# Sends of the negated maxima moved from ScalarE to SyncE, and the step tables of a fused attention kernel shifted

## The chip, the cores and the metric

The kernel runs on one core of a Trainium2 chip. Its engines are PE (TensorE, the matmuls; its weight loads are listed as PEld), DVE (VectorE), ACT (ScalarE), POOL (GpSimd) and SP (SyncE, here the engine that issues the transfers). Each works through its own list in order; semaphores tie the lists together. The metric is the device time of one execution in microseconds; lower is better.

## What is computed

Sixteen sequences of 128 rows and 256 columns go through two attentions and two feed-forward layers. The change touches the first attention, which works across columns: per sequence eight heads, each of 16 of the 128 rows.

```python
def _L0_xattn_ref(q, k, v):                 # q: layernorm(x); k = v = ctx_2048; 8 heads
    qh = q.reshape(b * h, d // h, m)
    kh = k.reshape(b * h, d // h, -1)
    vh = v.reshape(b * h, c // h, -1)
    qk = jnp.einsum('bdm,bdn->bmn', qh, kh) * scale
    sm = jax.nn.softmax(qk, axis=-1)
    ret = jnp.einsum('bmn,bcn->bcm', sm, vh)
x = x + _L0_xattn_ref(_layernorm(x), ctx_2048, ctx_2048)
x = x + _L0_ffn_ref(_layernorm(x), ...)     # 16 experts, top-k tokens for each
x = x + _L1_xattn_ref(_layernorm(x), ctx_2048, mask)
x = x + _L1_ffn_ref(_layernorm(x), ...)     # top-k rows, gelu
```

## The kernel before

A batch is one sequence, a unit is two batches (NU = 8 units), a step is one head of one batch: 16 steps to a unit, LAST = 128 steps in all. Stage A runs them. Each engine has its own unrolled loop over t, and in step t

- PE computes scores of step n = `ahead(t)` into `score_bank` (two matmuls; n is t + 24 from t = 16 on, two n per step for t of 8 to 15), then the transposed scores of step t + 2 into `scoret_bank` (`scores_t`, which waits for the exponential of step t), and every fourth step, after the exponential of step t, sixteen small matmuls for probabilities times values (`values`, into `pv_bank`). So scores of unit w start at PE's step 24, 40, 56, 72, 88 for w = 3 to 7, and step 12 for w = 2.
- DVE takes the row maximum of the scores of step n (`maximum`), and once per batch divides (`gather_parts`, `invert`, `bring_over`), makes statistics and scales rows.
- ACT does the exponential of step t from `scoret_bank` (`exponential`), then whatever copies are due.
- POOL does subtractions, roots and additions.

The transposed scores need the maxima as two extra rows of `q_stack`. PE transposes a batch's maxima (`max_t`) into `t0_bank`, ACT writes the high bf16 part of their negative (`neg_high`), DVE the low part (`neg_low`), and two DMAs carry both into `q_stack` (`send_neg_max`, L884 to L887). In before ACT issues these two DMAs itself, in its step MAX_T + 3, after waiting for `neg_low`. `scores_t` of a batch's first step waits for them (PE step 8b - 2).

The other input of the scores are stacks: q and k of a unit are each split into three bf16 parts. k: `high_k` on ACT, `rest_k` on POOL, `mid_k` on ACT, `low_k` on POOL. q: `scale_q` on DVE, `high_q`, `rest_q`, `mid_q`, `low_q` likewise. SP writes the parts to DRAM (`write_k_parts`, `write_q_parts`), fetches the next unit's rows (`load_stage`), waits until the parts are written and loads them back as stacks in nine DMAs (`load_stacks`). PE's first scores of a unit wait for these nine.

When each of these is due is set by hand, in tables of step numbers (L51 to L58): `MAX_T` for a batch's `max_t`, `STAGE` for `high_k`, `rest_k` and the statistics of a unit, `MID_K`, `SCALE_Q`, `HIGH_Q`, `MID_Q` for the splits, `CTX_T` and `TAKE_VT` for the transposed context. Each loop asks `due(table, t)`, with an offset of its own. In before SP has no steps: its order is unit by unit. Which engine reaches a step first is up to the semaphores; the tables fix only the order on each engine.

## Time and profile before

| | us |
|---|---|
| median of 3 runs (451.76 to 454.36) | 451.77 |
| the profiled execution, its time | 453.62 |
| its span on the core | 451.8 |
| PE busy in it | 293.6 (65%) |
| DVE busy | 298.2 (66%) |
| ACT busy | 170.7 (38%) |
| POOL busy | 113.1 (25%) |

The profile is one execution. Times are us from the start of the span unless marked ns; a row of the timeline is the start, the duration, the engine, the line of the kernel and output<-inputs, with the engine's idle time before it and what ended it in brackets. A "q" behind an engine's name is its sequencer, which issues DMAs. Stage A's exponentials run from 44.37 to about 266; a search for a threshold follows until about 326, then the second attention and the last layer. Line numbers are those of before, unless said otherwise.

### The profile page before, as it was taken

Reading aid. Unit: us, or ns where it says so; the run is one execution under the profiler, and the core shown is the slowest. Engines: PE = TensorE matmul, PEld = TensorE weight load, DVE = VectorE, ACT = ScalarE, POOL = GpSimd, SP = SyncE. Lnnn points to the kernel's source line nnn. Section 1 sums busy time; section 2 is a strip of 40 time slices with the busy share of each in tenths; the row PEclk is TensorE's granted clock in tenths of the full one; section 3 lists DMA queues with packets and bytes.
Section 4 is the critical chain, followed back from the end, with each engine's and each line's share of the span. In section 5 each row is a group of like instructions: output and inputs, shape, how many; then the busy total and the mean of one; then the engine's idle time right before and its main releaser. Section 6 shows DMA issues by size and latency. Waiting matters only on the chain.

```text
span 451.8 us, 6847 instructions
## 1 busy us (share of the span) xinstructions
PE 293.6 (65%) x1888; PEld 185.2 (41%) x1888; DVE 298.2 (66%) x925; ACT 170.7 (38%) x413; POOL 113.1 (25%) x248
## 2 busy tenths in 40 slices
PE   0053764777667878767986764100157999999996
PEld 0011422343333443434442422000135888888884
DVE  6855565457666875768775453888747788878641
ACT  3201632334554465534354651000011455565622
POOL 1101662233322434222122221000013333332300
PEclk9999966668888695899685995555555799999999
DMA  3876584662925719245000047000000000000001
GB/s 97 194 186 113 137 166 83 155 107 93 159 49 146 135 51 180 54 114 111 0 2 1 3 127 245 1 1 0 0 0 1 1 23 2 23 23 23 23 25 46
DMA packets 24106, 32.80 MB, mean 73 GB/s; under 512 B 3915, under 2 KB 22158, under 8 KB 22542
## 3 DMA queue, kind: packets, MB, share of 16 engines
q1 hardware_dynamic: 23566, 32.34, 31.4%
q10 hardware_dynamic: 512, 0.13, 0.2%
q8 instruction: 12, 0.20, 0.2%
q14 instruction: 16, 0.13, 0.1%
HBM read 23.88 MB, written 8.39 MB: 71 GB/s over the span
## 4 chain that ended last, share of the span: by engine, by line
DVE 33%; PE 33%; issue 11%; DMA 8%; ACT 5%; ACTq 4%; POOL 4%; SPq 2%; DVEq 1%; POOLq 0%
PE pv_bank L1054 7%; DVE row_max L574 6%; DVE denom_inv L592 5%; PE scoret_bank L1040 4%; ACTq L886 4%; DMA q_stack<-q_parts_dram 4%; PE t_bank L1237 4%; PE score_bank L1027 4%; PE pv_bank L1155 3%; ACT probs L875 2%; DMA q_parts_dram<-q_parts 2%; PE score_bank L1218 2%; POOL rstd L390 2%; DVE junk L685 1%; DVE denom_own L596 1%
## 5 line engine op out<-in xcount | busy, mean ns | idle before, releaser
L574 DVE TENSOR_REDUCE row_max<-score_bank 128x2 f32<-128x512 f32 x112 | 73.5, 675 | 65.0 <-PE score_bank L1027 64.6
L875 ACT ACTIVATE probs<-scoret_bank 128x512 f32<-128x512 f32 x128 | 74.2, 600 | 77.0 <-issue 50.8
L1040 PE MATMUL scoret_bank<-q_stack,k_stack 98*128 98x256 bf16 x256 | 61.1, 332 | 53.4 <-ACT probs L875 44.5
L1027 PE MATMUL score_bank<-k_stack,q_stack 96*128 96x256 bf16 x240 | 57.7, 337 | 23.3 <-DMA q_stack<-q_parts_dram 16.1
L1040 PEld LDWEIGHTS scoret_bank<-q_stack,k_stack 98*128 98x128 bf16 x256 | 24.8, 114 | 75.7 <-ACT probs L875 57.6
L1054 PE MATMUL pv_bank<-probs,values_ones 128*32 128x256 f32 x512 | 48.6, 514 | 0.0
L1027 PEld LDWEIGHTS score_bank<-k_stack,q_stack 96*128 96x128 bf16 x240 | 21.4, 114 | 56.5 <-DVE row_max L574 21.5
L388 POOL TENSOR_SCALAR var_eps<-mv 128x1 f32<-128x1 f32 x48 | 9.1, 190 | 137.1 <-DVE mv L743 78.3
L1155 PE MATMUL pv_bank<-q_stack,k_stack 128*128 (+1 forms) x256 | 35.8, 283 | 0.4 <-ACT q_stack L1003 0.4
L978 ACT COPY xnt<-score_bank 128x256 f32<-128x256 f32 x16 | 6.0, 373 | 75.4 <-PE score_bank L1176 75.4
L1155 PEld LDWEIGHTS pv_bank<-q_stack,k_stack 128*128 128x128 f32 x256 | 33.7, 201 | 1.3 <-issue 0.9
L404 POOL TENSOR_TENSOR x_new<-gathered,xs 128x256 f32<-128x256 f32 x16 | 11.6, 722 | 73.4 <-DVE gathered L599 68.4
L1237 PE MATMUL t_bank<-k_stack,probs 128*128 128x256 f32 x128 | 29.4, 382 | 0.0
L390 POOL TENSOR_TENSOR rstd<-var_eps,minus_half 128x1 f32<-128x1 f32 x48 | 26.3, 549 | 9.1 <-POOL var_eps L388 9.1
L592 DVE RECIPROCAL denom_inv<-gathered 128x256 f32<-128x256 f32 x16 | 27.9, 1744 | 0.1
L1237 PEld LDWEIGHTS t_bank<-k_stack,probs 128*128 128x128 f32 x128 | 23.7, 190 | 2.9
L1054 PEld LDWEIGHTS pv_bank<-probs,values_ones 128*32 128x32 f32 x512 | 16.3, 133 | 19.2 <-issue 15.0
L1136 PE MATMUL t_bank<-count,same_expert 128*128 128x3 bf16 x15 | 2.8, 186 | 31.8 <-DVE equal L685 31.8
L997 ACT ACTIVATE probs<-pv_bank,b1s 128x128 f32<-128x128 f32 x64 | 17.6, 379 | 11.8 <-PE pv_bank L1155 11.7
L1083 PE MATMUL t_bank<-wr_moving,xnt 128*128 128x272 f32 x64 | 18.6, 415 | 1.2 <-ACT xnt L927 1.2
L1070 PE MATMUL t_bank<-ident,ctx_stage 128*128 128x128 f32 x32 | 7.2, 367 | 16.2 <-DMA x_stage<-in_x_dram 16.2
L586 DVE SCALAR_TENSOR_TENSOR gathered<-pv_bank,high,low_part 128x512 f32<-128x512 f32 x16 | 11.9, 742 | 6.3 <-ACT low_part L921 6.3
(191 smaller groups left out, 542.2 us busy)
## 6 DMA issues: line engine op xcount, KB each, us to landing
q_stack<-q_parts_dram SPq DMA_DIRECT2D x48, 128.0 KB, 7.0
k_parts_dram<-k_parts SPq DMA_DIRECT2D x24, 128.0 KB
q_parts_dram<-q_parts SPq DMA_DIRECT2D x24, 128.0 KB
k_stack<-k_parts_dram SPq DMA_DIRECT2D x8, 384.0 KB, 4.9
ctx_stage<-in_ctx_dram SPq DMA_DIRECT2D x8, 256.0 KB, 3.3
x_stage<-in_x_dram SPq DMA_DIRECT2D x8, 256.0 KB, 4.2
k_stack<-k_parts_dram SPq DMA_DIRECT2D x8, 256.0 KB, 5.5
xs<-in_x_dram SPq DMA_DIRECT2D x8, 256.0 KB, 7.8
```

The lines of the kernel that those rows point to most:

```text
L390: pool.tensor_tensor(dst, work, minus_half[:, 0:dst.shape[1]], ALU.pow).then_inc(s[ready], 1)
L574: dve.tensor_reduce(row_max[:, i, :, h], score_bank[bank_of][:, :].rearrange("p (m n) -> p m n", m=2), AX.X, ALU.max).then_inc(s["max_done ...
L592: dve.reciprocal(denom_inv[:, i, :], gathered[:, i, 0, :]).then_inc(s["div_step"], 1)
L875: act.activation(probs[:, j % PROBS, :], scoret_bank[j % 2][:, :], ACT.Exp).then_inc(s["exp_done"], 1)
L886: act.dma_start(q_stack[QROWS + part:QROWS + part + 1, u % SLOTS, :, i, :], neg_max[:, i, part, :]).then_inc(neg_loaded[i], 16)
L997: act.activation(hid[:, h, :], hid_bank[h // 4][:, (h % 4) * P:(h % 4 + 1) * P], ACT.Gelu_apprx_tanh, bias=b1s[:, h:h + 1]).then_inc(s["f_ ...
L1027: ins = pe.matmul(to[:, m * D:(m + 1) * D], q_stack[0:QROWS, slot, h, b_in, m * P:(m + 1) * P], k_stack[0:QROWS, slot, h, b_in, :], start= ...
L1040: ins = pe.matmul(scoret_bank[j % 2][:, k * D:(k + 1) * D], k_stack[0:SROWS, slot, h, b_in, k * P:(k + 1) * P], q_stack[0:SROWS, slot, h, ...
L1054: ins = pe.matmul(pv_bank[i][pair * Q:(pair + 1) * Q, odd * D:(odd + 1) * D], values_ones[:, i, k, pair, odd, :], probs[:, (j - GROUP + 1 ...
L1083: pe.matmul(t1_bank[:, 0:D + NE], xnt[:, i, k, :], wr_moving[:, k, :], start=(k == 0), stop=False)
L1155: ins = pe.matmul(hid_bank[h // 4][:, (h % 4) * P:(h % 4 + 1) * P], w1s[:, k, h * P:(h + 1) * P], zg[:, k, bass.ds(P * t, P)], start=(k == ...
L1237: ins = pe.matmul(y_bank[:, 0:D], hid[:, h, :], w2s[:, h, :], start=(h == 0), stop=(h == NF - 1))
```

## The change

`send_neg_max` becomes a function of SP. SP's loop over units becomes a loop over the steps: it sends a batch's maxima two steps behind `neg_low`, writes k parts in step MID_K, writes q parts and loads the next unit's rows in step MID_Q, and loads the stacks two steps later. The tables get new numbers; the high and the low part of the maxima get tables of their own (`NEG_HIGH` for ACT, `NEG_LOW` for DVE).

```diff
-MAX_T = {1: 1, 2: 9, 3: 15, **{b: NH * b - 13 for b in range(4, NB)}}
-STAGE = {3: 9, 4: 21, **{w: STEPS * (w - 3) for w in range(5, NU)}}
-MID_K = {2: 0, 3: 11, 4: 23, **{w: STAGE[w] + 3 for w in range(5, NU)}}
-SCALE_Q = {2: 1, 3: 11, 4: 24, **{w: STAGE[w] + 6 for w in range(5, NU)}}
-HIGH_Q = {2: 3, 3: 13, 4: 25, **{w: STAGE[w] + 7 for w in range(5, NU)}}
-MID_Q = {2: 5, 3: 15, 4: 27, **{w: STAGE[w] + 9 for w in range(5, NU)}}
-CTX_T = {2: 5, 3: 12, 4: 23, **{w: STAGE[w] + 7 for w in range(5, NU)}}
-TAKE_VT = {2: 7, 3: 13, 4: 25, **{w: STAGE[w] + 9 for w in range(5, NU)}}
+MAX_T = {1: 0, 2: 9, 3: 16, 4: 21, **{b: NH * b - 14 for b in range(5, NB)}}
+NEG_HIGH = {b: MAX_T[b] + 3 for b in MAX_T} | {1: 1}
+NEG_LOW = {b: MAX_T[b] + 2 for b in MAX_T} | {1: 1, 2: 10}
+STAGE = {3: 10, 4: 22, 5: 35, 6: 50, 7: 66}
+MID_K = {2: 0, **{w: STAGE[w] + 3 for w in STAGE}}
+SCALE_Q = {2: 0, 3: 12, 4: 25, 5: 40, 6: 55, 7: 71}
+HIGH_Q = {2: 4, **{w: SCALE_Q[w] + 4 for w in STAGE}}
+MID_Q = {w: HIGH_Q[w] + 3 for w in HIGH_Q}
+CTX_T = {2: 4, 3: 13, 4: 31, 5: 39, 6: 55, 7: 71}
+TAKE_VT = {2: 6, 3: 15, 4: 34, 5: 42, 6: 58, 7: 74}
...
-            sp.wait_ge(neg_loaded[0], 32)
+            send_neg_max(0, 0)
             load_x(0)
             load_small()
...
+            for t in range(LAST):
+                for b in due(NEG_LOW, t - 2):
+                    send_neg_max(b // 2, b % 2)
+                for w in due(MID_K, t):
+                    write_k_parts(w)
+                for w in due(MID_Q, t):
+                    write_q_parts(w)
+                    if w + 1 < NU:
+                        load_stage(w + 1)
+                for w in due(MID_Q, t - 2):
+                    load_stacks(w, w >= SLOTS)
+                if t % STEPS == STEPS - 4 and t // STEPS + 1 < NU:
+                    wait_apart(sp, s["x_loaded"], 16 * (t // STEPS + 1))
+                    load_x(t // STEPS + 1)
...
# POOL
-                for w in due(STAGE, t - 1):
+                for w in due(STAGE, t + 1):
                     rest_k(w)
...
-                for w in due(MID_Q, t - 1):
+                for w in due(MID_Q, t + 1):
                     low_q(w)
...
# DVE
-                        if t == NH * b + 11:
+                        if t == NH * b + 10:
                             gather_parts(b, i)
...
-                    for b in due(MAX_T, t - 2):
+                    for b in due(NEG_LOW, t):
                         neg_low(b, b % 2)
...
# ACT
-            send_neg_max(0, 0)
...
-                    if t == NH * b + 24:
+                    if t == NH * b + 26:
                         take_yw(b)
...
-                    if t == NH * b + 21:
+                    if t == NH * b + 23:
                         take_xnt(b, i, b < 2)
-                for b in due(MAX_T, t - 1):
+                for b in due(NEG_HIGH, t):
                     neg_high(b, b // 2, b % 2)
-                for b in due(MAX_T, t - 3):
-                    send_neg_max(b // 2, b % 2)
...
# PE
-                    if t == NH * b + 22:
+                    if t == NH * b + 23:
                         yw(b, b % 2)
```

Likewise on DVE `invert`, `bring_over`, `stats_x1` and `scale_rows` come one step earlier, on POOL `rest_q` and `low_k` as `low_q`, and `fill_values` one step later.

ScalarE (ACT) around the middle q part of unit 7 (q_parts<-q_rest), before. probs is the exponential, neg_max the high part and its send, vt, low_part, xnt and y_ext the copies of `take_vt`, `take_even`, `take_xnt` and `take_yw`:

```order
L875 ACTIVATE probs<-scoret_bank 128x512
L891 COPY vt<-t_bank 128x512
L914 CAST q_parts<-q_rest 128x512
L875 ACTIVATE probs<-scoret_bank 128x512
L920 ACTIVATE low_part<-pv_bank,low 128x256
L921 ACTIVATE low_part<-pv_bank,low 128x256
L875 ACTIVATE probs<-scoret_bank 128x512 x2
L881 ACTIVATE neg_max<-t_bank 8x256
L875 ACTIVATE probs<-scoret_bank 128x512
L927 COPY xnt<-t_bank 128x256
L875 ACTIVATE probs<-scoret_bank 128x512
L886 DMA q_stack<-neg_max 1x8x256 x2
```

The same place of after:

```order
L894 COPY y_ext<-t_bank 128x272
L918 ACTIVATE low_part<-pv_bank,low 128x256
L919 ACTIVATE low_part<-pv_bank,low 128x256
L889 COPY vt<-t_bank 128x512
L879 ACTIVATE probs<-scoret_bank 128x512
L908 CAST q_parts<-qn 128x512
L879 ACTIVATE probs<-scoret_bank 128x512 x2
L885 ACTIVATE neg_max<-t_bank 8x256
L879 ACTIVATE probs<-scoret_bank 128x512
L912 CAST q_parts<-q_rest 128x512
L879 ACTIVATE probs<-scoret_bank 128x512
L925 COPY xnt<-t_bank 128x256
```

The DMA row is gone. The middle q part stood five exponentials ahead of the send and ahead of the high part; now it stands one exponential behind the high part, and the copy to xnt one behind that.

SyncE (SP) from the k parts of unit 5 to its stacks, before; k_parts_dram and q_parts_dram are the writes, the stage rows the next unit's inputs:

```order
L273 DMA k_parts_dram<-k_parts 8x16x512 x3
L279 DMA q_parts_dram<-q_parts 8x16x512 x3
L264 DMA ctx_stage<-in_ctx_dram 128x2x256
L265 DMA x_stage<-in_x_dram 128x2x256
L294 DMA k_stack<-k_parts_dram 48x4096
L295 DMA k_stack<-k_parts_dram 32x4096
L296 DMA k_stack<-k_parts_dram 16x4096
L298 DMA q_stack<-q_parts_dram 16x4096 x6
L268 DMA xs<-in_x_dram 128x2x256
```

After, from the k parts of unit 5 as well:

```order
L281 DMA k_parts_dram<-k_parts 8x16x512 x3
L270 DMA xs<-in_x_dram 128x2x256
L275 DMA q_stack<-neg_max 1x8x256 x2
L287 DMA q_parts_dram<-q_parts 8x16x512 x3
L266 DMA ctx_stage<-in_ctx_dram 128x2x256
L267 DMA x_stage<-in_x_dram 128x2x256
L302 DMA k_stack<-k_parts_dram 48x4096
L303 DMA k_stack<-k_parts_dram 32x4096
L304 DMA k_stack<-k_parts_dram 16x4096
L306 DMA q_stack<-q_parts_dram 16x4096 x6
```

A send of two small DMAs, and the load of xs, now stand between the k parts' and the q parts' write. Each of the other sends has such a place between the bulk transfers.

GpSimd (POOL) around the low q part of unit 6 (q_parts<-q_rest), before:

```order
L378 TENSOR_TENSOR q_rest<-qn,q_parts 128x512
L388 TENSOR_SCALAR var_eps<-mv 128x1
L390 TENSOR_TENSOR rstd<-var_eps,minus_half 128x1
L407 COPY xs<-x_new 128x256
L383 TENSOR_TENSOR q_parts<-q_rest,q_parts 128x512
L436 COPY values_ones<-vt 128x8x16 x2
```

After:

```order
L382 TENSOR_TENSOR q_rest<-qn,q_parts 128x512
L440 COPY values_ones<-vt 128x8x16 x2
L387 TENSOR_TENSOR q_parts<-q_rest,q_parts 128x512
L408 TENSOR_TENSOR x_new<-gathered,xs 128x256
```

In before the root and the copy of a batch (var_eps, rstd, xs) stand between the q rest and the low q part; in after only the filling of the values does.

## Rows read from the trace of the kernel before

**Rows 1.** The page, section 4: the chain that ended last, by engine

```profile
DVE 33%; PE 33%; issue 11%; DMA 8%; ACT 5%; ACTq 4%; POOL 4%; SPq 2%; DVEq 1%; POOLq 0%
```

**Rows 2.** Windows: length, busy us of PE, PEld, DVE, ACT, POOL; clock, DMA

```profile
59.00:74.00 15.00, 7.49 (x44) 3.77 (x45) 7.81 (x17) 4.66 (x10) 6.18 (x9) 0.59 0.86 150
97.76:130.27 32.51, 22.30 (x152) 11.31 (x151) 21.43 (x42) 14.79 (x33) 11.21 (x19) 0.81 0.53 110
130.27:240.34 110.07, 83.84 (x596) 43.71 (x594) 78.37 (x150) 53.03 (x117) 31.82 (x62) 0.81 0.39 81
215.60:240.34 24.74, 18.93 (x128) 9.94 (x125) 18.95 (x36) 10.40 (x23) 4.74 (x12) 0.78 0.01 1
```

**Rows 3.** Waits from 130.27 to 240.34: who for whom, us, times, longest

```profile
DVE row_max L574 <- PE score_bank L1027: 29.4, 11, 4.0
PE scoret_bank L1040 <- ACT probs L875: 23.0, 15, 2.7
ACT probs L875 <- issue: 32.9, 8, 5.1
```

**Rows 4.** Timeline of one batch: start, us, engine, line, what [idle]

```profile
198.52 0.41 DVE L579 SCALAR_TENSOR_TENSOR neg_max<-t_bank,neg_max 8x256 bf16<-8x256 f32 x1
...
198.96 1.29 ACTq L886 DMA_DIRECT2D q_stack<-neg_max  x2
...
200.30 1.08 ACT L875 ACTIVATE probs<-scoret_bank 128x512 f32<-128x512 f32 x2 [5.11 <-issue]
...
202.93 0.61 PE L1027 MATMUL score_bank<-k_stack,q_stack 96*128 96x256 bf16 x2
...
203.65 0.69 DVE L574 TENSOR_REDUCE row_max<-score_bank 128x2 f32<-128x512 f32 x1 [3.52 <-PE score_bank L1027]
```

**Rows 5.** Timeline, unit 4: middle q part to stack loads

```profile
106.09 0.64 ACT L914 CAST q_parts<-q_rest 128x512 bf16<-128x512 f32 x1
...
108.09 1.80 SPq L279 DMA_DIRECT2D q_parts_dram<-q_parts  x3
...
110.45 0.47 SPq L265 DMA_DIRECT2D x_stage<-in_x_dram  x1
...
112.91 0.33 SPq L294 DMA_DIRECT2D k_stack<-k_parts_dram  x1
...
115.25 2.92 SPq L298 DMA_DIRECT2D q_stack<-q_parts_dram  x6
```

**Rows 6.** Timeline, first maxima of units 3, 5, 7; steps behind unit 5

```profile
101.39 0.69 DVE L574 TENSOR_REDUCE row_max<-score_bank 128x2 f32<-128x512 f32 x1 [4.80 <-PE score_bank L1027]
...
160.81 0.39 PE L1027 MATMUL score_bank<-k_stack,q_stack 96*128 96x256 bf16 x2
...
161.31 0.69 DVE L574 TENSOR_REDUCE row_max<-score_bank 128x2 f32<-128x512 f32 x1 [2.34 <-PE score_bank L1027]
...
164.07 0.59 PEld L1054 LDWEIGHTS pv_bank<-probs,values_ones 128*32 128x32 f32 x16 [0.22 <-issue]
...
166.21 0.60 ACT L875 ACTIVATE probs<-scoret_bank 128x512 f32<-128x512 f32 x1
...
215.94 0.69 DVE L574 TENSOR_REDUCE row_max<-score_bank 128x2 f32<-128x512 f32 x1 [2.86 <-PE score_bank L1027]
```

**Rows 7.** Timeline, unit 2 arrives; step 19; `values` at half clock

```profile
71.91 1.03 PE L1027 MATMUL score_bank<-k_stack,q_stack 96*128 96x256 bf16 x4 [6.38 <-DMA q_stack<-q_parts_dram]
...
86.19 1.08 ACT L875 ACTIVATE probs<-scoret_bank 128x512 f32<-128x512 f32 x2 [2.17 <-issue]
...
87.80 1.94 PE L1054 MATMUL pv_bank<-probs,values_ones 128*32 128x256 f32 x16
```

**Rows 8.** The page: queue, packets; us to landing, median; spread

```profile
q10 hardware_dynamic: 512, 0.13, 0.2%
...
x_stage<-in_x_dram SPq DMA_DIRECT2D x8, 256.0 KB, 4.2
...
DMA to landing us min/median/max: 5.7/7.0/9.3
```

More of the change, by code:

```diff
@@ L268, in load_x, with send_neg_max @@
                 sp.dma_start(xs[:, bass.ds(2 * u, 2), :], x_rows[:, bass.ds(2 * u, 2), :]).then_inc(s["x_loaded"], 16)
+            def send_neg_max(u, i):
+                sp.wait_ge(s["neg_done"], 2 * u + i + 1)
+                for part in range(2):
+                    sp.dma_start(q_stack[QROWS + part:QROWS + part + 1, u % SLOTS, :, i, :],
+                                 neg_max[:, i, part, :]).then_inc(neg_loaded[i], 16)
             def write_k_parts(u):
@@ L620, in stage_a @@
                         i = b % 2
-                        if t == NH * b + 16:
+                        if t == NH * b + 15:
                             stats_x1(b, i)
-                        if t == NH * b + 18:
+                        if t == NH * b + 17:
                             scale_rows(b, i, b < 2)
+                        if t == NH * b + 10:
+                            gather_parts(b, i)
                         if t == NH * b + 11:
-                            gather_parts(b, i)
+                            invert(b, i)
                         if t == NH * b + 12:
-                            invert(b, i)
-                        if t == NH * b + 13:
                             bring_over(b, i)
-                    for w in due(STAGE, t if t < STEPS * 2 else t - 1):
+                    for w in due(STAGE, t + 1 if t < STEPS * 2 else t):
                         stats_q(w)
@@ L881, in neg_high @@
                 act.mul(neg_max[:, i, 0, :], t0_bank[0:NH, 0:D], -1.0).then_inc(s["neg_hi"], 1)
-            def send_neg_max(u, i):
-                act.wait_ge(s["neg_done"], 2 * u + i + 1)
-                for part in range(2):
-                    act.dma_start(q_stack[QROWS + part:QROWS + part + 1, u % SLOTS, :, i, :],
-                                  neg_max[:, i, part, :]).then_inc(neg_loaded[i], 16)
             def take_vt(u):
@@ L939, in _ @@
             neg_high(0, 0, 0)
-            send_neg_max(0, 0)
             high_k(2)
-            for t in range(LAST + 3 * NH + 2):
+            for t in range(LAST + 3 * NH + 3):
                 if t < LAST:
```

24 lines of the change are left out of this document (4 added, 20 removed).

## The prediction

> **What bounds the kernel now.** I read the page first, then the windows and waits of the stage of the 128 steps, then its timeline. No engine is full: the chain that ended last goes through DVE 33%, PE 33%, "issue" 11%, and 4% at ACTq, ScalarE's sequencer [rows 1]. 4% of the span of 451.8 us is 18 us, spent where nothing is computed.
>
> The stretch 130.27 to 240.34 holds 64 steps, eight batches: 110.07 us, or 13.76 for 8 steps, with VectorE busy only 78.37, PE 83.84 at a granted clock of 0.81, ScalarE 53.03 [rows 2]. The waits in it form a ring: VectorE waits 29.4 us in 11 waits for PE's scores, PE 23.0 in 15 for ScalarE's exponential, and ScalarE stands 32.9 us in 8, one per batch, before an exponential, put down to "issue" [rows 3]. The timeline of a batch shows the knot. Behind its divisions VectorE comes to the low part of the negated maxima at 198.52; ScalarE's next instruction is the send, which waits for it and takes 1.29 us; only then comes the exponential of 200.30, after 5.11 us without one. PE does transposed scores and `values` and reaches the next scores at 202.93, and VectorE's next maximum starts at 203.65 after 3.52 us of idleness [rows 4]. So VectorE, send, exponential, `values`, scores, VectorE: a ring of latencies, not the work of an engine.
>
> **The change, term by term.** The sends first. Taken off ScalarE, they take with them 1.29 us of issue per batch and the wait for VectorE. SyncE's issues per unit, nine stack loads, six writes and three more, take about 0.33 to 0.6 us each [rows 5], some 10 us in a unit of 27; four more small ones fit. What is left is the engines' own work for 8 steps, VectorE 78.37/8 = 9.8 us, PE 83.84/8 = 10.5. If nothing else bound, a batch would take about 11.5, a us above PE's work for the handovers that stay, and not 13.76.
>
> Second, the middle and low q parts are made later, in steps. MID_Q goes from 15, 27, 41, 57, 73 (units 3 to 7) to 19, 32, 47, 62, 78. The scores of these units start at PE's step 24, 40, 56, 72, 88, so 9, 13, 15, 15, 15 steps of lead become 5, 8, 9, 10, 10. Into them must fit a chain that waits on transfers: middle q part on ScalarE, low part on POOL, three writes, the wait until written, nine loads, the landing. Unit 4's in before: 106.09 middle part, 108.09 first write, 112.91 first load, last six loads issued from 115.25 over 2.92 us, so the last at about 117.7 [rows 5]; the median landing of such a load is 7.0 us, from 5.7 to 9.3 [rows 8]. That is 124.7, or 18.6 us from the middle part. Unit 4's second load took longer than the others to issue, about 1 us between the rows; I take **17.5** (bounds 16.3 with the landing of 5.7, 20.0 with 9.3). In before the lead hid all of it.
>
> So I expect the stage to be paced unit by unit: scores of a unit start, some steps to the next unit's middle q part, 17.5 us, that unit's scores start. The steps between, from tables: six from unit 5's scores to unit 6's middle part (56 to 62), six again for unit 7, seven for unit 5 (40 to 47), eight for unit 4 (24 to 32). In before six steps from unit 5's first maximum at 161.31 to the start of an exponential at 166.21 took 4.9 us, at the full clock [rows 6]. Behind a stall PE may be at half clock: its clock was 0.59 in 59 to 74, where it stood for unit 2's stacks [rows 2, 7], 16 `values` matmuls take 1.94 and not 1.07, a pair of scores 0.61 and not 0.39 [rows 4, 6, 7]. Five PE steps with one `values` are then 10 x 0.22 + 0.87 = 3.1 us longer, so 4.9 to 8.0, plus 0.6 for the exponential. I take **7.5** for six steps, 9 for seven, 10 for eight.
>
> The start: unit 2's scores wait for their stacks until 71.91, 6.38 us [rows 7]. Their middle part stands two steps later, but ScalarE loses a send ahead of it; I leave 71.9 (bounds -1, +1). From there unit 3's middle part is at step 19. In before that step's exponential started at 86.19, behind a send and 2.17 us of standing [rows 7]; without them 84.0. 84.0 + 0.6 + 17.5 is **102.1** for unit 3's scores. In before its first maximum was at 101.39 [rows 6], scores some 0.5 earlier: 1.2 late.
>
> The sum: unit 3's scores at 102.1; unit 4's at 102.1 + 10 + 17.5 = 129.6; unit 5's at 129.6 + 9 + 17.5 = 156.1 (before 160.8); unit 6's at + 25.0 = 181.1; unit 7's at 206.1 (before 215.94 - 0.5 = 215.4) [rows 6], **9.3 us early**. Behind unit 7 there is no stack to wait for. The two batches from 215.60 to 240.34 took 24.74 us with VectorE busy 18.95 [rows 2]; I give back the issue of their two sends, **2.6 us**, and not the whole gap, since PE's busy time of 18.93 there, in order behind both neighbours, leaves less to win. The last 24 steps have one send: **0.3**. Tail and all behind it: the same work in the same order, 0. Sum 9.3 + 2.6 + 0.3 = **12.2 us**.
>
> Terms counted at nothing. (a) `high_k` of the next unit stands three steps behind MID_Q (four for unit 7), and its rows are loaded behind the q parts' write: second load issued at 110.45, landing 4.2 [rows 5, 8], 8.6 us after the middle part of 106.09, against some 5 us of steps. ScalarE, and VectorE at the statistics, stand 3 to 4 us, and behind them the next exponentials and maxima. It is hidden inside the 17.5; were the stacks faster it would cost up to 3 per unit. (b) VectorE's `neg_low`, its step 8b-12, now waits for a high part of ScalarE's step 8b-11. VectorE runs behind ScalarE there and finds it done; without that cover it is an exponential, 0.60 [rows 6], per batch. (c) PE's `max_t` waits for `take_vt` of the same step, which stands behind two other copies, at most about two exponentials' time, once per unit, with the next scores queued behind it. It falls into the steps between and is in the 7.5. (d) Batch 3's maxima are sent behind unit 3's q write and two loads, some 84 + 2 + 3, landing near 92, and PE's step 22 needs them: a wait of some 4 us, but the stacks for step 24 come only at 102.
>
> At (d) two queues matter. The row shows before's sends on a queue of their own, q10, with 512 packets [rows 8]. The Trainium skill, "DMA: Bandwidth & Descriptors", Queues, rings and completion order, says that an engine takes one ring's descriptors in order and goes round between rings; on SyncE's ring a send would stand behind all bulk ahead of it. By that rule each send next to a stack load lands up to a load's length later, which speaks against the change (R4 below). And the Trainium skill, "TensorE: Matmul & The Clock Gate", HAM oscillation, says that waits for transfers leave the matmuls behind them at half rate; the trace agrees with `values` at 1.94 after the stall of 71.91. By it six steps cost the 8.6 at the upper end, and the sum would be four times about 1 us less, 8 us.
>
> **Rivals.** *R1, the stacks stay hidden* (chain below 15 us). Then PE and VectorE pace the stage at 11.5 for 8 steps: the ten batches from 97.76 to 240.34 took 32.51 + 110.07 = 142.6 us [rows 2], now 3 x 12.5 + 7 x 11.5 = 118: 24.6 saved, 427. Against it: even the shortest landing makes the chain 16.3. *R2, nothing moves*: the chain takes 19.4 us and the steps between 10.3, 9.3, 8, 8. Unit 3's scores start at 104.0, unit 7's at 104.0 + 29.7 + 28.7 + 27.4 x 2 = 217.2, 1.8 late, against 2.9 saved behind: 450.7. *R3, slower*, by unit 3's stacks: if its middle part comes at 87 and not 84 (PE at half clock through steps 14 to 19) and the chain takes 20.0, unit 3's scores start at 107.6, and with units 30.3, 29.3, 28 and 28 apart unit 7's at 223.2, 7.8 late: 451.8 + 7.8 - 2.9 = 456.7. It decides from a chain of about 19.8 us on. *R4, the maxima*: a send made in step 8b-12 is needed in PE's step 8b-2, ten steps or some 15 us later, against at most 10 us of issue and 9.3 of landing of the bulk in front. A few us per unit; I count it into R2.
>
> **How the numbers follow.** The profiled execution's span, 451.8, and the median of the three runs, 451.77, are the same (its own time was 453.62): 451.8 - 12.2 = 439.6. Chances: the forecast, paced by the stacks with 6 to 18 us gained, 0.50, with a range of its own of 434 to 446; R1 0.20; R2 with R4 0.17; R3 0.13. For 8 in 10 I go from 429 to 453, which leaves out half of R1 and most of R3. About 1%, 4.5 us, is what a measurement of this kernel can tell from no change. Faster than that: 0.50 + 0.20 + 0.02 of R2 = 0.72. Same: 0.15 of R2 and 0.02 of R3 = 0.17. Slower: the other 0.11 of R3.
>
> **What would show it.** In the profile of after no ACTq row stands in the chain, and ScalarE's stand of 4 us before an exponential once per batch is gone. PE waits for q_stack<-q_parts_dram at the starts of units 3 to 7, 3 to 9 us each; none would be R1, more than 9 R2 or R3. POOL's low q part starts within 1 us of the middle part's end, the first load about 4.8 us after the first write. Unit 3's first maximum is near 102.6, unit 7's near 206.6. My account of before is wrong if VectorE still waits 3 us per batch with no transfer behind it: then the ring closes through another instruction than the send.

## The result, and the profile after

The changed kernel took 450.0 us (median of 20 executions) against 452.8 us for the kernel before; the ratio over matched executions is 0.989, interval 0.986 to 0.993. By the ratio that is 5 us gained of the 12.2 forecast; the time lies inside the range of 429 to 453 and 10 us above the forecast of 439.6. Executions of after go from 444.1 us (mean granted clock 0.830) to 459.4 (0.777). Ratios are taken over the faster executions of both kernels, and the profiled one of after, 454.4 us at 0.798, is not among those. So a size read from its trace alone need not hold for a typical execution.

The first row below is the chain that ended last in after, by engine. Then waits: of PE in the whole execution, and of ACT and DVE from 130 to 230 us (who for whom, us, times, longest).

```profile
DVE 29%; PE 28%; DMA 15%; issue 12%; SPq 5%; POOL 5%; ACT 4%; DVEq 1%; POOLq 0%; ACTq 0%
...
PE score_bank L1022 <- DVE row_max L578: 29.4, 31, 4.2
PE score_bank L1022 <- DMA q_stack<-q_parts_dram: 20.1, 5, 9.5
PE scoret_bank L1035 <- DMA q_stack<-neg_max: 11.4, 2, 7.4
...
ACT probs L879 <- PE scoret_bank L1035: 47.5, 27, 4.7
PEld score_bank L1022 <- DVE row_max L578: 24.0, 27, 2.2
DVE row_max L578 <- PE score_bank L1022: 23.6, 7, 4.0
```

ACTq has gone from 4% to 0, and ScalarE's eight stands put down to "issue" [rows 3] are no longer there. In their place ScalarE waits for PE's transposed scores, up to 4.7 us at a time, DVE still waits up to 4.0 us for scores, and transfers have grown from 8% of the chain to 15%.

PE's waits for transfers in stage A behind unit 2 (timeline: start, us, engine, line, what, idle before it and what ended it):

```profile
91.32 0.59 PE L1035 MATMUL scoret_bank<-q_stack,k_stack 98*128 98x256 bf16 x2 [4.00 <-DMA q_stack<-neg_max]
101.19 0.61 PE L1022 MATMUL score_bank<-k_stack,q_stack 96*128 96x256 bf16 x2 [4.90 <-DMA q_stack<-q_parts_dram]
127.97 0.39 PE L1022 MATMUL score_bank<-k_stack,q_stack 96*128 96x256 bf16 x2 [0.33 <-DMA q_stack<-q_parts_dram]
182.12 0.39 PE L1022 MATMUL score_bank<-k_stack,q_stack 96*128 96x256 bf16 x2 [0.20 <-DMA q_stack<-q_parts_dram]
```

The scores of units 3 and 4 start at 101.2 and 128.0, where 102.1 and 129.6 were forecast. But the forecast had PE wait 3 to 9 us for the stacks of each of units 3 to 7, and only unit 3's wait is of that size. Units 4 and 6 waited 0.33 and 0.20 us; the stacks of units 5 and 7 landed 0.6 and 1.3 us before PE came for them. So something else keeps nearly the same pace, and it was not in the forecast. The timeline of after around step 103 shows it, one batch of eight:

```profile
219.34 1.94 PE L1049 MATMUL pv_bank<-probs,values_ones 128*32 128x256 f32 x16
...
221.20 2.18 PE L1078 MATMUL t_bank<-wr_moving,xnt 128*128 128x272 f32 x4
...
223.32 0.40 PE L1080 MATMUL t_bank<-bias_parts,ones_bf 3*128 3x272 bf16 x1
...
223.65 0.61 PE L1022 MATMUL score_bank<-k_stack,q_stack 96*128 96x256 bf16 x2
...
224.37 1.47 DVE L578 TENSOR_REDUCE row_max<-score_bank 128x2 f32<-128x512 f32 x2 [4.00 <-PE score_bank L1022]
...
224.72 0.60 ACT L879 ACTIVATE probs<-scoret_bank 128x512 f32<-128x512 f32 x1 [4.68 <-PE scoret_bank L1035]
```

The diff moves `yw`, the router's matmuls, from PE's step 8b + 22 to 8b + 23. That is step 7 of an eight, where `values` stands too. PE now does both in one piece, 219.34 to 223.65, 4.3 us without a score for anyone, and DVE (4.00) and ScalarE (4.68) stand for it. The same row of idleness was 3.52 and 5.11 in before, behind the send [rows 4]: a pause of the same length, once per eight steps.

Windows (length; busy us of PE, PEld, DVE, ACT, POOL; granted clock, DMA share, GB/s) of after, steps 88 to 104 and the last 24 steps; then the same of before. Each window starts and ends at an exponential, so that the same steps lie in both.

```profile
203.60:230.93 27.33, 22.25 (x146) 11.23 (x146) 18.60 (x35) 12.18 (x26) 4.58 (x12) 0.75 0.15 26
230.93:264.80 33.87, 27.88 (x167) 12.07 (x167) 15.78 (x30) 16.98 (x36) 6.54 (x16) 0.66 0.03 9
```

```profile
213.74:240.34 26.60, 20.63 (x146) 10.75 (x146) 18.95 (x36) 11.78 (x27) 4.74 (x12) 0.78 0.01 1
240.34:266.10 25.76, 20.49 (x162) 9.28 (x163) 12.60 (x24) 16.75 (x38) 5.77 (x15) 0.83 0.01 1
```

Steps 88 to 104 took 27.3 us against 26.6, and the last 24 took 33.9 against 25.8, at a granted clock of 0.66 against 0.83. (The window of 24.74 us in [rows 2] starts at 215.60, 1.9 us behind the exponential of step 88, and is not the same stretch.) At step 104 after was 9.4 us ahead of before (230.93 against 240.34), and it ended stage A behind it. The first maximum of unit 7 and the first instruction behind stage A, in after:

```profile
210.73 0.69 DVE L578 TENSOR_REDUCE row_max<-score_bank 128x2 f32<-128x512 f32 x1 [3.99 <-PE score_bank L1022]
...
282.09 0.42 DVE L666 TENSOR_REDUCE lg_max<-y_ext 128x16 f32<-128x256 f32 x1 [4.24 <-ACT y_ext L894]
```

and in before:

```profile
281.48 0.42 DVE L662 TENSOR_REDUCE lg_max<-y_ext 128x16 f32<-128x256 f32 x1 [4.24 <-ACT y_ext L896]
```

5.2 us ahead at 210.73 (before 215.94, [rows 6]), 0.6 behind at 282.09. What follows stage A takes 170.4 us in either trace. In this trace the gain was made and then given back, most of it in the last 24 steps.

### The profile page after: what moved, and what is told of

Same layout as the page of the kernel before. It is cut to its first block, busy times and chain, and to the rows that moved or that the text cites. A ratio compares the mean times of both kernels' runs of the same rounds, so it can differ in the third digit from the quotient of the medians.

```text
span 452.5 us, 6847 instructions
## 1 busy us (share of the span) xinstructions
PE 296.0 (65%) x1888; PEld 186.5 (41%) x1888; DVE 298.9 (66%) x925; ACT 171.9 (38%) x413; POOL 112.8 (25%) x248
## 4 chain that ended last, share of the span: by engine, by line
DVE 29%; PE 28%; DMA 15%; issue 12%; SPq 5%; POOL 5%; ACT 4%; DVEq 1%; POOLq 0%; ACTq 0%
DMA q_stack<-q_parts_dram 9%; PE pv_bank L1049 5%; DVE row_max L578 4%; PE t_bank L1078 4%; DMA q_parts_dram<-q_parts 4%; PE score_bank L1022 4%; DVE denom_inv L596 3%; PE scoret_bank L1035 3%; PE pv_bank L1150 3%; PE t_bank L1232 2%; SPq L306 2%; PE score_bank L1213 2%; POOL rstd L394 2%; DMA q_stack<-neg_max 2%; DVE junk L689 1%
## 5 line engine op out<-in xcount | busy, mean ns | idle before, releaser
L1022 PE MATMUL score_bank<-k_stack,q_stack 96*128 96x256 bf16 x240 | 55.4, 324 | 49.8 <-DVE row_max L578 29.4
L1035 PE MATMUL scoret_bank<-q_stack,k_stack 98*128 98x256 bf16 x256 | 58.6, 321 | 21.3 <-DMA q_stack<-neg_max 11.4
L1022 PEld LDWEIGHTS score_bank<-k_stack,q_stack 96*128 96x128 bf16 x240 | 19.3, 107 | 76.9 <-DVE row_max L578 47.4
L1049 PE MATMUL pv_bank<-probs,values_ones 128*32 128x256 f32 x512 | 47.2, 502 | 0.7 <-ACT probs L879 0.7
L1035 PEld LDWEIGHTS scoret_bank<-q_stack,k_stack 98*128 98x128 bf16 x256 | 25.8, 112 | 37.2 <-ACT probs L879 16.5
L1078 PE MATMUL t_bank<-wr_moving,xnt 128*128 128x272 f32 x64 | 27.5, 569 | 1.0 <-ACT xnt L925 1.0
L596 DVE RECIPROCAL denom_inv<-gathered 128x256 f32<-128x256 f32 x16 | 27.9, 1744 | 0.1
L1078 PEld LDWEIGHTS t_bank<-wr_moving,xnt 128*128 128x128 f32 x64 | 15.4, 266 | 14.3 <-issue 10.0
## 6 DMA issues: line engine op xcount, KB each, us to landing
q_stack<-q_parts_dram SPq DMA_DIRECT2D x48, 128.0 KB, 7.1
k_parts_dram<-k_parts SPq DMA_DIRECT2D x24, 128.0 KB
q_parts_dram<-q_parts SPq DMA_DIRECT2D x24, 128.0 KB
```

Source lines behind the costliest of these rows:

```text
L596: dve.reciprocal(denom_inv[:, i, :], gathered[:, i, 0, :]).then_inc(s["div_step"], 1)
L1022: ins = pe.matmul(to[:, m * D:(m + 1) * D], q_stack[0:QROWS, slot, h, b_in, m * P:(m + 1) * P], k_stack[0:QROWS, slot, h, b_in, :], start= ...
L1035: ins = pe.matmul(scoret_bank[j % 2][:, k * D:(k + 1) * D], k_stack[0:SROWS, slot, h, b_in, k * P:(k + 1) * P], q_stack[0:SROWS, slot, h, ...
L1049: ins = pe.matmul(pv_bank[i][pair * Q:(pair + 1) * Q, odd * D:(odd + 1) * D], values_ones[:, i, k, pair, odd, :], probs[:, (j - GROUP + 1 ...
L1078: pe.matmul(t1_bank[:, 0:D + NE], xnt[:, i, k, :], wr_moving[:, k, :], start=(k == 0), stop=False)
```

## The experiments

Fourteen kernels ran, each beside the kernel before, whose median was 452.7 to 453.6 each time. Ratios are to before, with 95% intervals.

**e1: yw back at its step.** `take_xnt`, which feeds it, goes back with it.

```diff
-                    if t == NH * b + 23:          # PE: yw
+                    if t == NH * b + 22:
-                    if t == NH * b + 23:          # ACT: take_xnt
+                    if t == NH * b + 21:
```

> The changed kernel with PE's yw back from step 8b+23 to 8b+22 and ScalarE's take_xnt from 8b+23 to 8b+21; all else as changed. In the changed kernel yw's 1.08 to 2.18 us of matmuls and its bias matmul stand right behind the 1.07 to 1.94 us of values (step 7 of each eight), and VectorE (4.00 us) and ScalarE (4.68 us) both stand idle until the next scores, once per batch. Theory A (the block of values and yw closes a new ring on PE): parting them moves yw into the time in which PE waits for VectorE's reciprocal anyway, so 1 to 2 us per batch for 14 batches, ratio to before 0.955 to 0.970, and the idle time of VectorE before its first maximum of a batch falls from 4.0 to under 3. Theory B (the stage is paced by the late stacks, as predicted): nothing moves, 0.985 to 0.993. Theory C (PE's granted clock decides and the order doesn't): also 0.985 to 0.993, with the mean clock unchanged.

443.5 us, 0.977 (0.972 to 0.982). The step of `yw` costs the changed kernel 1.2 points, 5.5 us, in A's direction but less than A had it. VectorE's idle time before the first maximum of a batch, 4.0 us in after, is 0.56 at 223.04 in e1. What shows in its place are the stacks; waits of PE, and the timeline at unit 7:

```profile
PE score_bank L1022 <- DMA q_stack<-q_parts_dram: 26.7, 5, 9.4
...
212.98 0.61 PE L1022 MATMUL score_bank<-k_stack,q_stack 96*128 96x256 bf16 x2 [6.87 <-DMA q_stack<-q_parts_dram]
```

**e2: the kernel before with nothing changed but the sends.** SyncE gets `send_neg_max` and the loop over steps; tables and offsets are those of before.

```diff
 # ACT
-                for b in due(MAX_T, t - 3):
-                    send_neg_max(b // 2, b % 2)
 # SP, loop over t
+                for b in due(MAX_T, t - 4):
+                    send_neg_max(b // 2, b % 2)
```

> The kernel before with one part of the change: the sends of the maxima are issued by SyncE, which goes by steps; all tables and the offsets of PE, VectorE, ScalarE and POOL as before. If the sends on ScalarE were the ring (prediction), this part alone gives 1.3 us of issue and the wait per batch back: ratio 0.955 to 0.975, and ScalarE's standing of 4 to 5 us before an exponential goes. If another wait stands right behind it (rival: gathered parts, roots and the transposed rows wait in its place), 0.985 to 1.0. No stack is late here, 13 to 15 steps of lead, so the prediction's stack pacing plays no part.

438.6 us, 0.965 (0.959 to 0.971): 16 us, three times what the whole change brought. The ring of before went through the send, as the prediction read it from [rows 4]. What is left of waits shows where the send went:

```profile
PE scoret_bank L1033 <- DMA q_stack<-neg_max: 28.5, 7, 9.1
PE scoret_bank L1033 <- ACT probs L877: 22.4, 23, 4.1
PE score_bank L1020 <- DMA q_stack<-q_parts_dram: 14.8, 2, 9.1
```

PE waited 8.9 us in 2 for the maxima in before and 28.5 in 7 here. With the tables of before a send comes to SyncE behind a unit's nine stack loads. The Trainium skill, "DMA: Bandwidth & Descriptors" (Queues, rings and completion order), says that each DMA engine takes the descriptors of a ring in ring order; a send issued behind the nine loads then stands behind them. These waits agree with it, though no run here gave the sends a ring of their own on SyncE.

**e3: the kernel before with nothing changed but yw, at 8b + 23.**

```diff
-                    if t == NH * b + 22:          # PE: yw
+                    if t == NH * b + 23:
```

> The kernel before with one number of the change: PE's yw in step 8b+23 and not 8b+22. Theory A: yw then stands behind values, on the ring of before too (exponential, values, scores, VectorE), and adds its 1.3 to 2.6 us to each of 14 batches, ratio 1.02 to 1.06. Theories B and C: it only moves within PE's idle time, 1.00.

490.9 us, 1.083 (1.078 to 1.087): 37 us lost, 2.7 us in each of 14 eights, more than A expected. Its timeline has both pauses in a row: PE waits 2.71 us for the exponential behind the send, then does `values` for 1.94 and `yw` for 2.18.

```profile
236.46 0.61 PE L1040 MATMUL scoret_bank<-q_stack,k_stack 98*128 98x256 bf16 x2 [2.71 <-ACT probs L875]
237.00 1.94 PE L1054 MATMUL pv_bank<-probs,values_ones 128*32 128x256 f32 x16
238.87 2.18 PE L1083 MATMUL t_bank<-wr_moving,xnt 128*128 128x272 f32 x4
```

**e4: the changed kernel with the parts of units 3 to 7 one to three steps earlier.** MID_K, HIGH_Q and MID_Q follow from these two tables.

```diff
-STAGE = {3: 10, 4: 22, 5: 35, 6: 50, 7: 66}
-SCALE_Q = {2: 0, 3: 12, 4: 25, 5: 40, 6: 55, 7: 71}
+STAGE = {3: 9, 4: 20, 5: 33, 6: 48, 7: 64}
+SCALE_Q = {2: 0, 3: 10, 4: 22, 5: 37, 6: 53, 7: 69}
```

> The changed kernel with the parts of units 3 to 7 made 2 to 4 steps earlier (STAGE 9, 20, 33, 48, 64, SCALE_Q 10, 22, 37, 53, 69, and MID_K, HIGH_Q and MID_Q with them); yw stays in step 8b+23. Theory B (late stacks pace the stage): 2 to 3 steps or 3 to 4 us per unit come back, ratio 0.955 to 0.970. Theory A: only unit 3's wait of 4.9 us and the 4.0 us for the maxima of batch 3 can come back, 0.975 to 0.985.

449.9 us, 0.992 (0.988 to 0.995), no gain. I took this for the end of B at the time. It was too quick: in its trace the exponential of step 24 comes at 103.5 us against 92.2 in after, and from there to step 127 it needs 15 us less (157.1 against 172.2). Of these 15 some 4 may be no effect of the edit, since after's profiled execution lies 4.4 us above its median and e4's at its own. Two effects of opposite sign stand in this kernel; e9 and e12 go back to before's tables, where the early start is kept (step 24 at 94.3 and 91.5).

**e5: the changed kernel with yw one step later still, 8b + 24,** apart from `values` again.

```diff
-                    if t == NH * b + 23:          # PE: yw
+                    if t == NH * b + 24:
```

> The changed kernel with one edit: yw on PE one step later, at 8b + 24 instead of 8b + 23 (take_yw stays at 26). There it is again apart from the values of step 7 of each eight: the scores of the next step stand between them. Theory A (values and yw directly behind each other keep PE from the scores for 4.3 us in each eight steps, and DVE and ACT stand for it): the stall of 4.9 to 5.3 us after exponential 8b + 1 goes, as in e1, ratio to before 0.970 to 0.985. Rival D (what costs is only that yw is later than the step at which the rest expects it, so that later still is worse): 0.995 to 1.02.

448.4 us, 0.990 (0.986 to 0.993), the same as after. So the neighbourhood with `values` is not the point by itself. The timeline shows one pause turned into two: ScalarE waits 2.19 us for its exponential, and then 0.93 us before its step 26, in which it copies `yw`'s result, because `yw` has only just ended:

```profile
230.46 0.60 ACT L879 ACTIVATE probs<-scoret_bank 128x512 f32<-128x512 f32 x1 [2.19 <-PE scoret_bank L1035]
...
231.99 0.39 ACT L894 COPY y_ext<-t_bank 128x272 f32<-128x272 f32 x1 [0.93 <-PE t_bank L1080]
```

Behind a batch's division DVE's row maxima come late, and PE's scores of step 8b + 23 wait for them: 1.12 us in e5 at 239.19, 1.13 in after at 218.38 and in e12 at 209.20. With `yw` at 8b + 22 (e9, 208.97) it is done inside this gap and the wait is gone. At 23 and 24 it comes behind the gap, when DVE and ScalarE stand for PE.

**e6: e1 with e4's tables.** Its edit is those of e1 and e4 together.

> e1 (yw back at 8b + 22) together with e4's tables (STAGE and SCALE_Q of units 3 to 7 one to three steps earlier). Theory A with B behind it (once the ring of yw is open, late stacks pace: in e1 exponentials at a unit's end wait 8.9, 5.7, 4.3, 5.4 and 4.4 us, with 11.4 us of waits of PE for the stacks between 130 and 230 us): ratio 0.950 to 0.968, 430 to 438 us. Rival E (the stacks are not the bound, or earlier parts take from ACT and DVE what they give): 0.975 to 0.990, as e1 or worse.

438.7 us, 0.971 (0.966 to 0.976): between the two expectations, with the same late start as e4 (step 24 at 101.5).

**e7: e2 with yw at 8b + 23.** The edit is e3's.

> e2 (before with only the sends moved to SP) and yw at 8b + 23. It prices yw behind values where no send holds ACT and the tables are those of before. Theory A: the pause of 4 us returns in each eight steps, of which e2's slack hides a part: e3 showed 2.7 us an eight (38 us in 14) beside the sends' pause, the changed kernel against e1 only 7 us; so ratio 1.00 to 1.05. Rival F (yw's price came only from lying behind the send's pause, and nothing is lost without it): 0.960 to 0.975, as e2.

452.6 us, 0.999 (0.995 to 1.003). Against e2 that is 14 us, all of what moving the sends had won. The copy of `yw`'s result still stands at ScalarE's step 24 here; waits from 130 to 230 us:

```profile
ACT y_ext L892 <- PE t_bank L1078: 31.1, 8, 5.2
```

ScalarE stands 3.9 us in each eight for PE's `yw`. In the changed kernel that copy is at 26 and this wait is gone, and the step costs 5.5 us and not 14. That the later copy is the reason was not tested by itself; other tables differ too.

**e8: e2 with DVE's operations of a batch one step forward.**

```diff
-                        if t == NH * b + 16:      # stats_x1; scale_rows 18 -> 17
+                        if t == NH * b + 15:
-                        if t == NH * b + 11:      # gather; invert 12 -> 11, bring_over 13 -> 12
+                        if t == NH * b + 10:
```

> e2 and DVE's operations of a batch one step forward (gather 10, invert 11, bring_over 12, stats_x1 15, scale_rows 17), which is the changed kernel's order on DVE; tables and yw as in before. It prices that part alone. My forecast counted it at nothing: 0.960 to 0.972, as e2. Rival G (the gap between e1, 0.977, and e2, 0.965, comes from DVE's gather standing for ACT's low part one step too early, 13.1 us in 4 in the changed kernel): 0.973 to 0.985.

429.4 us, 0.948 (0.943 to 0.954), 7 to 9 us below e2. The forecast had counted this part of the change at nothing, and its rival G was a loss. PE's waits for the maxima fall from 28.5 to 21.9 us; over 130 to 230 us the granted clock is 0.95 and not 0.86. Windows of e8, then of e2:

```profile
130.00:230.00 100.00, 77.22 (x662) 41.78 (x653) 83.18 (x158) 61.15 (x132) 31.87 (x66) 0.95 0.43 92
```

```profile
130.00:230.00 100.00, 75.86 (x595) 40.67 (x592) 77.74 (x148) 53.35 (x115) 30.90 (x61) 0.86 0.44 90
```

**e10: e8 with ScalarE's takes of the changed kernel.**

```diff
-                    if t == NH * b + 24:          # take_yw
+                    if t == NH * b + 26:
-                    if t == NH * b + 21:          # take_xnt
+                    if t == NH * b + 23:
```

> e8 with take_xnt at 8b + 23 and take_yw at 8b + 26 on ACT, as in the changed kernel; yw stays at 22 (it then waits for the transposed rows that ACT takes one step ahead of where yw needs them, at PE step 22 against ACT step 23: PE runs two steps ahead in scores_t, so the copy comes late). Expected if ACT's later takes cost nothing: 0.940 to 0.955, as e8; if they are a ring of their own (PE's yw at 22 stands for the copy at 23): 0.97 to 1.01.

434.3 us, 0.962 (0.955 to 0.969): 1.4 points, 6 us lost, between the two expectations.

**e9: e1 with the parts' tables of before.** STAGE, MID_K, SCALE_Q, HIGH_Q, MID_Q and the offsets of POOL and DVE that go with them.

```diff
-STAGE = {3: 10, 4: 22, 5: 35, 6: 50, 7: 66}
+STAGE = {3: 9, 4: 21, **{w: STEPS * (w - 3) for w in range(5, NU)}}
-MID_Q = {w: HIGH_Q[w] + 3 for w in HIGH_Q}
+MID_Q = {2: 5, 3: 15, 4: 27, **{w: STAGE[w] + 9 for w in range(5, NU)}}
 ...
-                for w in due(MID_Q, t + 1):       # POOL: low_q
+                for w in due(MID_Q, t - 1):
```

> e1 (the changed kernel with yw at 8b + 22) with the tables STAGE, MID_K, SCALE_Q, HIGH_Q and MID_Q of before, and POOL's and DVE's offsets for them. The maxima's tables (MAX_T, NEG_HIGH, NEG_LOW), CTX_T and TAKE_VT stay those of the changed kernel. e8 (sends and DVE's step forward, nothing else of the change) measured 0.948 and e1 0.977: 13 us lie between them. Theory H (the q parts, made four to six steps later in the changed kernel, cost most of these 13 us, by PE's waits for the stacks, 26.7 us in 5 in e1 and 14.3 in 2 in e8): 0.945 to 0.962. Rival I (the 13 us lie in the other moved parts, the maxima's tables or ACT's later take_yw): 0.970 to 0.985.

431.4 us, 0.950 (0.943 to 0.957). The parts made later cost e1 2.7 points, 12 us: theory H. PE's waits for the stacks fall from 26.7 us to 15.4 in 2, but those for the maxima rise from 12.3 in 2 to 21.4 in 7, so the waits on PE alone do not add up to the 12 us.

**e11: e8 with the parts of units 5, 6, 7 two to four steps earlier than in before.**

```diff
-STAGE = {3: 9, 4: 21, **{w: STEPS * (w - 3) for w in range(5, NU)}}
+STAGE = {3: 9, 4: 21, 5: 30, 6: 44, 7: 60}
```

> e8 with STAGE of units 5, 6, 7 at 30, 44, 60 instead of 32, 48, 64 (MID_K to MID_Q with them; CTX_T and TAKE_VT stay). In e8 PE still waits 14.3 us in 2 for the stacks and 21.9 us in 7 for the maxima, whose sends stand on SP behind the nine loads of a unit's stacks. Theory H (late stacks and the sends behind them are the next bound): about half of those 36 us is paid, so 0.925 to 0.942, 419 to 427 us. Rival E (earlier parts only move ACT's waits for x_stage): 0.943 to 0.960.

424.3 us, 0.936 (0.929 to 0.943): the fastest version, 29 us below before. PE's waits for the maxima are 17.9 us in 2 instead of 21.9 in 7, and those for the stacks as before (14.4 in 2). In the trace the first send behind the loads of units 5 to 7 is issued 1.5 to 3.6 us after them, in e8 0.6 us, which I take for the reason; it was not tested apart.

**e12: the changed kernel with e9's edit alone,** `yw` at 8b + 23.

> The changed kernel with only e9's edit to the parts' tables and offsets undone; yw stays at 8b + 23 and take_xnt at 8b + 23. It says how the two losses combine. On the changed kernel e1 (yw alone back) gave 1.2 percentage points and e4 (some parts one to three steps earlier) nothing; on e1 the parts' tables gave 2.7. Theory J (the later of two paces: with yw at 23 its pause sets the eight steps, so parts made in time give nothing): ratio to before 0.980 to 0.992. Rival K (the losses add): 0.955 to 0.970.

436.2 us, 0.960 (0.953 to 0.967): K, the losses add, and the parts' tables are the larger one, 13 us. Between e9 and e12, which differ only in `yw` and `take_xnt`, lie 1.0 points, 5 us, the same price as e1's. Its trace also shows what goes with the clock. Windows of e12 over steps 88 to 96 and 96 to 104, and PE's timeline in the second:

```profile
197.30:208.10 10.80, 8.20 (x73) 4.61 (x73) 9.04 (x18) 6.04 (x13) 2.30 (x6) 1.00 0.08 27
208.10:219.00 10.90, 8.19 (x73) 4.61 (x73) 9.14 (x19) 6.13 (x14) 2.29 (x6) 1.00 0.01 2
...
209.74 1.07 PE L1049 MATMUL pv_bank<-probs,values_ones 128*32 128x256 f32 x16
210.74 1.18 PE L1078 MATMUL t_bank<-wr_moving,xnt 128*128 128x272 f32 x4
```

No parts are made in these steps, and the order on each engine is that of after. At a clock of 1.00 (2.4 GHz) eight steps take 10.8 or 10.9 us, with `values` and `yw` in 2.2; in after they take 13.7 at 0.75, with both at the 1.2 GHz rate in 4.1. e9 has the same stretch with `yw` at 22:

```profile
209.20:218.70 9.50, 7.97 (x74) 4.61 (x73) 9.07 (x18) 5.96 (x14) 2.35 (x6) 1.00 0.01 3
```

So `yw`'s step costs 1.4 us an eight at the full clock and some 2.8 more in after's trace, where the clock falls on it. Of the 20 us between the spans of after and e12, 12 lie in steps 88 to 127. The medians lie only 14 us apart, since after's profiled execution is 4.4 us above its median and e12's 1.9 below.

**e13: the changed kernel with nine spare matmuls an eight on PE,** where it stands for DVE.

```diff
+                if STEPS < t < LAST and t % NH in (5, 6):
+                    spare(t, 4 if t % NH == 5 else 5)   # 256 columns each, into the free half of pv_bank
```

> The changed kernel with nine spare matmuls an eight of steps on PE: four of 256 columns after its step 8b + 5 and five after 8b + 6, where PE stands 0.8 and 1.1 us for DVE's row maxima; they write the half of pv_bank that values fills next, nothing reads them, and no order or wait changes. Theory C' (yw directly behind values is dear because the granted clock falls just there: steps 88 to 104 took 13.7 and 13.6 us at 0.75 in the changed kernel, 10.8 and 10.9 us at 1.00 in e12, where the same instructions stand in the same order; PE's waits before bring the clock down): with PE kept busy the clock holds over values and yw, the eight takes 10.9 to 12 us, and the whole 0.955 to 0.980. Rival L (the clock follows the pauses and does not make them; the parts' tables cost e12's 13 us by themselves): the spare work, 0.9 us an eight, is hidden or adds, 0.985 to 1.01.

448.6 us, 0.996 (0.992 to 1.000): no gain, L by the number. In the trace steps 88 to 96 took 15.8 us, with a wait of 3.7 for unit 7's stacks; from step 96 on the clock did hold. The last 24 steps of e13, beside 33.87 at 0.66 of after:

```profile
230.10:255.80 25.70, 20.60 (x193) 11.45 (x192) 14.88 (x29) 16.41 (x36) 6.58 (x16) 1.00 0.04 11
```

The two profiled executions are unlike: e13's took 444.2, 4.4 us below its median, and after's 454.4, 4.4 above. So the 8 us between these stretches are no measure of what the spare matmuls bring; by the medians it is 1.4 us, by the ratios a loss of 3.

**e14: e11 with the same spare matmuls,** which prices them.

> e11 with the same spare matmuls. In e11 yw stands at 8b + 22 and the granted clock between 102 and 232 us is 0.95 already, so there is little to win: 0.93 to 0.945 under either theory, above 0.945 if the spare work costs by itself.

430.2 us, 0.958 (0.953 to 0.963). Where the clock is high already, the spare work costs 6 us by the medians and 10 by the ratios; in e13 it brought 1 or cost 3 by the same two measures. If it costs the changed kernel as much, the steadier clock gave back some 7 us in e13 (6 + 1, or 10 - 3). That rests on two kernels with different tables and was not shown directly.

## Why the prediction was half right

One chain of kernels leads from before to after, each step one part of the change. At 453 us a point is 4.5 us:

| step | from | to | us |
|---|---|---|---|
| sends to SyncE | 1 | 0.965 (e2) | -16 |
| DVE's operations one step forward | 0.965 | 0.948 (e8) | -7 |
| ScalarE's takes later | 0.948 | 0.962 (e10) | +6 |
| maxima's and context's tables, `fill_values`; take_xnt back | 0.962 | 0.950 (e9) | -5 |
| parts' tables and POOL's offsets | 0.950 | 0.977 (e1) | +12 |
| yw and take_xnt at 8b + 23 | 0.977 | 0.989 (after) | +5 |

The sum is -5 by construction, since each row starts where the last one ends. The intervals are about 0.6 points to either side, so rows of 5 us are not much larger than their error, and the fourth holds four things that no run separates. A price also depends on what it stands beside: `yw`'s step cost 5 us twice (e1 to after, e9 to e12), but 14 between e2 and e7.

*The ring of before: right.* "VectorE, send, exponential, `values`, scores, VectorE": e2 moved the sends alone and took 16 us, and ACTq's 4% of the chain is gone. The prediction also named a sign that this account is wrong: VectorE still waiting 3 us per batch with no transfer behind it. That sign came (4.0 us), but e2 answers it: the new wait goes through `yw`, which the same change had moved.

*Late stacks as the next pace: right in part, both terms of the wrong size.* e9 and e12 put 12 and 13 us on the parts' tables. Unit by unit, the forecast was steps between, then a chain of 17.5 us from the middle part to the landing. In the trace of after (us; forecast, measured):

| unit | steps between | chain | scores start |
|---|---|---|---|
| 3 | | 17.5, 18.7 | 102.1, 101.2 |
| 4 | 10, 8.4 | 17.5, 18.3 | 129.6, 128.0 |
| 5 | 9, 6.7 | 17.5, 19.3 | 156.1, 154.5 |
| 6 | 7.5, 5.8 | 17.5, 21.8 | 181.1, 182.1 |
| 7 | 7.5, 5.8 | 17.5, 20.8 | 206.1, 210.0 |

The starts of units 4 to 6 came within 1.6 us partly by luck: the steps between were 1.6 to 2.3 us shorter and the chain 0.8 to 4.3 longer than forecast. One reason for the chain is that the prediction took the median landing of all loads, 7.0, where the last of a unit's loads counts. That one landed 7.7 to 9.0 us after its issue in units 3 to 7 of after, and 7.2 to 8.4 in before. Timeline of unit 6's middle and low part:

```profile
160.29 0.61 ACT L912 CAST q_parts<-q_rest 128x512 bf16<-128x512 f32 x1
...
161.08 1.15 POOL L387 TENSOR_TENSOR q_parts<-q_rest,q_parts 128x512 bf16<-128x512 f32 x1 [0.99 <-ACT q_parts L912]
```

And the chain of waits through its stacks (start, us, what):

```profile
162.51 0.34 DVE neg_max L583
...
162.87 0.63 SPq L275
...
163.54 0.63 SPq L275
...
164.22 0.61 SPq L287
...
165.52 3.71 DMA q_parts_dram<-q_parts
...
173.07 9.01 DMA q_stack<-q_parts_dram
182.12 0.41 PE score_bank L1022 x2
```

The write of the q parts stands on SyncE behind a send, and the send waits for DVE's `neg_low`, which ends at 162.85, and takes 1.35 us to issue, though POOL had the low part at 162.2. The move past SyncE's queue that was to cost nothing ("four more small ones fit") put VectorE's work ahead of `neg_low` into the stacks' chain. It held the write for 2.0 us in units 6 and 7 and 0.7 in unit 5, not at all in units 3 and 4.

Unit 7 did not wait for its stacks. They landed at 208.7, 2.6 us after the forecast, and PE came at 210.0. The chain that ended last goes there through VectorE, scores, `values` and `yw`:

```profile
190.11 0.33 DVE neg_max L583
...
192.13 1.87 PE pv_bank L1049 x16
193.99 2.11 PE t_bank L1078 x4
...
205.76 1.86 PE pv_bank L1049 x16
207.63 2.11 PE t_bank L1078 x4
209.74 0.33 PE t_bank L1080
210.07 0.54 PE score_bank L1022 x2
```

So a unit took 26.6, 27.6 and 27.9 us in units 5 to 7, where 26.5, 25.0 and 25.0 were forecast, and unit 7's scores came about 4 us late.

*Behind unit 7: the step that failed most.* "Tail and all behind it: the same work in the same order, 0", and 2.6 us given back for two sends. From unit 7's first maximum to the end of stage A before took 65.5 us (215.94 to 281.48) and after 71.4 (210.73 to 282.09): 5.8 lost where 2.9 were to be won, so 8.7 of the 12.9 us between the forecast of 439.6 and this trace's span of 452.5. The other 4.1 are unit 7's. What lies behind stage A did cost the same (170.4 us); the loss is in the last steps of stage A. The order there was not the same. `yw` had moved behind `values`, which the diff shows in one line and the prediction gave no term; e1, e3 and e7 price it at 5.5, 37 and 14 us over the whole kernel. That the place of `yw` lengthens these steps is shown by e1 against after and by e9 against e12. (The window called two batches, 215.60 to 240.34, starts 1.9 us late; no term of the sum hangs on it.)

The size of 8.7 us is that of one execution, which had a lower clock than most of after, and a typical one was not profiled. In other kernels with `yw` at 23 the last 24 steps took 26.3 us at a clock of 0.95 (e4), 26.6 at 0.94 (e12), 31.1 at 0.84 (e7) and 37.5 at 0.56 (e3); in those with `yw` at 22, before included, 23.8 to 27.3 at 0.83 to 1.00. So `yw` behind `values` can go with a low clock there, but does not have to.

*Parts counted at nothing.* DVE's step forward was worth 7 to 9 us, and ScalarE's later takes cost 6. (d), the wait of some 4 us for batch 3's maxima, came as 4.00 us at 91.32. (a) stayed hidden inside the chain.

*The clock term: nearer by luck.* The prediction took from the Trainium skill, "TensorE: Matmul & The Clock Gate" (HAM oscillation), that waits for transfers leave the matmuls behind them at half rate, and weighed it at 8 us of gain instead of 12. The trace agrees behind unit 3's wait of 4.90 us, where the eight steps between took 8.4 us at a clock of 0.74. Behind the starts of units 4, 5 and 6, with hardly a wait, they ran at 1.00 and took 6.7, 5.8 and 5.8 us; six steps of 8.6 came nowhere. The result of 5 us is nearer to 8 than to 12 for another reason, the time lost to `yw` and to the longer chain. Nor is the `values` at 87.80 of [rows 7] good evidence for the stall at 71.91: it stands 16 us behind it. In after's last 40 steps the clock fell with no transfer waited for.

What stays open: how much of the 13 us of the parts' tables is the stacks' lateness and how much the clock that follows it. Against the trace of after, e12 has 12 of its 20 us in steps where no parts are made; e13 and e14 together hint at 7 us for the clock, and no kernel held the one fixed and moved the other. Open too is how much of the tail's 8.7 us a typical execution of after had.

## What to carry to other kernels

When a change moves many steps at once, write down for every engine what each moved instruction now stands directly behind, and give each a term, also those whose line in the diff looks incidental; here the line that moves `yw` cost 5 us, and 14 or 37 in other surroundings. Put matmuls whose result is not needed at once where PE stands anyway, not behind the gap. When several loads must all have landed, take the landing of the last one and not the median. And a queue that is given a waiting instruction makes all that is behind it wait for the same thing: the send on SyncE no longer held the exponentials, but it held the stacks' write by up to 2.0 us.

## What the runs showed of the hardware

Over steps 88 to 104 the same instructions in the same order ran at two paces: 13.7 us an eight at a mean granted clock of 0.75 in the profiled execution of after, and 10.8 at 1.00 in e12. In the slow one the clock went between its two levels once per eight, low over `values` and `yw` (1.94 and 2.18 us) and high over the steps with PE's short waits. Nine spare matmuls an eight (e13) went with a clock of 1.00 over the last 24 steps, 25.7 us instead of 33.9, between two executions that lie 4.4 us below and above their kernels' medians; at a clock already high (e14) they cost 6 us of 424 by the medians, 10 by the ratios. Small transfers issued on SyncE behind a unit's nine stack loads made PE wait up to 9.1 us (e2).
